# Attention scores from fp16 halves of q and k in the head loop of a decoder kernel

## What is computed

```
qkv = layernorm(x) @ w_qkv            # 16 heads of 128
scores = q @ k.T / sqrt(128)          # per sequence and head, 256 x 256
x = x + (softmax(scores) @ v) @ w_o
```

## Time and profile before

| | |
|---|---|
| median of 3 runs | 919.81 us (917.97 to 923.12) |
| time of the profiled execution | 922.4 us |
| its span, first to last instruction | 920.4 us |
| TensorE busy | 853.7 us (93%) |
| VectorE busy | 720.4 us (78%) |
| ScalarE busy | 535.1 us (58%) |
| GpSimd busy | 368.4 us (40%) |
| mean granted TensorE clock | 0.988 |
| head loop | from about 66 to 553 us of the span |

### The profile page before, as it was taken

How to read it: one execution, slowest core, us unless ns; L and a number is a source line. 1 busy time by engine, 2 the same in 40 slices (tenths; PEclk the granted TensorE clock), 3 DMA queues, 4 the chain that set the end, 5 groups by cost and what they waited for, 6 DMA issues and landing times. The chain is left out here.

```text
span 920.4 us, 18709 instructions
## 1 busy us (share of the span) xinstructions
PE 853.7 (93%) x6868; PEld 634.0 (69%) x6868; DVE 720.4 (78%) x1759; ACT 535.1 (58%) x1277; POOL 368.4 (40%) x354
## 2 busy tenths in 40 slices
PE   4788988999999999999999998999988889999786
PEld 3455766777777777777777776887855578787554
DVE  5748878878888788778887775897698779876885
ACT  1435576655665666556655744555566864545576
POOL 4103456545554455455555554043233031521410
PEclk9989999999999999999999998999999999999999
DMA  9123231011101110111000000000000010000001
GB/s 280 36 71 69 54 96 35 2 35 35 34 0 34 34 34 6 28 34 34 18 16 11 1 1 1 1 2 1 1 2 1 1 47 1 1 1 1 2 1 46
DMA packets 34722, 25.56 MB, mean 28 GB/s; under 512 B 9492, under 2 KB 31596, under 8 KB 34668
## 3 DMA queue, kind: packets, MB, share of 16 engines
q1 hardware_dynamic: 34380, 24.56, 10.3%
q10 hardware_dynamic: 288, 0.26, 0.1%
HBM read 22.65 MB, written 2.17 MB: 27 GB/s over the span
## 5 line engine op out<-in xcount | busy, mean ns | idle before, releaser
L483 POOL CAST exp_hi<-exp_scores 128x1024 f16<-128x1024 f32 x64 | 67.0, 1047 | 212.9 <-ACT exp_scores L596 212.9
L485 POOL TENSOR_TENSOR exp_lo<-exp_scores,exp_hi 128x1024 f16<-128x1024 f32 x64 | 140.7, 2199 | 5.1
L596 ACT ACTIVATE exp_scores<-banks,exp_bias,unscale 128x256 f32<-128x256 f32 x256 | 141.0, 560 | 2.1
L75 PE MATMUL banks<-value_out_hi,xn_t_hi 128*128 128x256 f16 x512 | 139.6, 273 | 0.3 <-DVE X L931 0.3
L76 PE MATMUL banks<-value_out_lo,xn_t_hi 128*128 128x256 f16 x512 | 139.6, 273 | 0.0
L77 PE MATMUL banks<-value_out_hi,xn_t_lo 128*128 128x256 f16 x512 | 139.6, 273 | 0.0
L1124 PE MATMUL banks<-qk 128*128 128x256 f32 x512 | 121.6, 380 | 9.0 <-ACT exp_scores L596 8.9
L1124 PEld LDWEIGHTS banks<-qk 128*128 128x128 f32 x512 | 96.6, 190 | 30.3 <-issue 9.6
L931 DVE SCALAR_TENSOR_TENSOR X<-banks,colsum,X 128x256 f32<-128x256 f32 x256 | 106.2, 477 | 11.0 <-DVE colsum L922 9.6
L575 ACT ACTIVATE qk<-banks 128x512 f32<-128x512 f32 x128 | 75.8, 601 | 57.9 <-PE banks L77 57.9
L906 DVE TENSOR_REDUCE neg_rowmax<-banks 128x4 f32<-128x1024 f32 x64 | 78.2, 1221 | 27.9 <-PE banks L1124 27.9
(11 more groups left out here) (253 smaller groups left out, 1973.9 us busy)
## 6 DMA issues: line engine op xcount, KB each, us to landing
head_weights<-in_wqkv_d SPq DMA_DIRECT2D x32, 128.0 KB, 3.7
weight_absmax_rows<-across_partitions SPq DMA_DIRECT2D x15, 256.0 KB, 4.0
X<-in_x_d SPq DMA_DIRECT2D x4, 512.0 KB, 7.3
head_weights<-in_wqkvt_d SPq DMA_DIRECT2D x16, 128.0 KB, 3.5
head_weights<-in_w_o_d SPq DMA_DIRECT2D x16, 128.0 KB, 3.5
out<-X SPq DMA_DIRECT2D x8, 256.0 KB, 2.1
ternary_then_kv_and_rows<-in_c_fc_d SPq DMA_DIRECT2D x1, 1024.0 KB, 6.2
ternary_then_kv_and_rows<-in_c_proj_d SPq DMA_DIRECT2D x1, 1024.0 KB, 8.0
```

Source lines behind the costliest of these rows:

```text
L75: nc.tensor.matmul(out, lhs[0], rhs[0], start=first, stop=False)
L483: nc.gpsimd.tensor_copy(probh[:, s1_.par], prob[:, s1_.par]).then_inc(exph_ready, 1)
L485: nc.gpsimd.tensor_tensor(probl[:, s1_.par], prob[:, s1_.par], probh[:, s1_.par], ALU.subtract).then_inc(expl_ready, 1)
L596: last = nc.scalar.activation(prob[:, s1_.par, t, :], sc_ps[t // ST][:, t % ST, :], ACT.Exp, bias=nbias[:, t:t + 1], scale=unscale[:, s1_. ...
```

## The change

The tile `qk` (fp32, double) is replaced by `qkh` and `qkl` (fp16, double) and a single fp32 tile `q_rows`. The scores become three fp16 products for each of the 4 tiles. ScalarE writes the upper half of q, a full copy of q into `q_rows`, and the upper half of k. GpSimd makes the lower half of q from `q_rows` and `qkh`. VectorE makes the lower half of k from PSUM and `qkh`. The semaphore `qk_ready` is split in four. TensorE's q product of the next step waits for `q_copied`, its k product for `k_lo`, and the scores wait for `q_lo` and `k_lo`.

```diff
-    qk = sb("qk", [P, 2, 2, NPAIR])
+    qkh = sb("qk_hi", [P, 2, 2, NPAIR], F16)
+    qkl = sb("qk_lo", [P, 2, 2, NPAIR], F16)
+    q_rows = sb("q_rows", [P, NPAIR])
...
-    qk_ready = sem("qk_ready")
+    qk_hi, q_copied, q_lo, k_lo = sem("qk_hi_ready"), sem("q_copied"), sem("q_lo_ready"), sem("k_lo_ready")
...
(GpSimd, after weights_lo, ahead of the halves of the exponentials)
+            if runs(i, 0):
+                pool.wait_ge(q_copied, i + 1)
+                nc.gpsimd.tensor_tensor(qkl[:, st.par, 0, :], q_rows[:, :], qkh[:, st.par, 0, :],
+                                        ALU.subtract).then_inc(q_lo, 1)
...
(ScalarE)
-                for s in range(2):
-                    act.wait_ge(qk_full, i * 2 + s + 1)
-                    nc.scalar.activation(qk[:, st.par, s, :], qk_ps[s], ACT.Copy).then_inc(qk_ready, 1)
+                act.wait_ge(qk_full, i * 2 + 1)
+                nc.scalar.activation(qkh[:, st.par, 0, :], qk_ps[0], ACT.Copy).then_inc(qk_hi, 1)
+                if not known(i) or i >= 1:
+                    act.wait_ge(q_lo, i)
+                nc.scalar.activation(q_rows[:, :], qk_ps[0], ACT.Copy).then_inc(q_copied, 1)
+                act.wait_ge(qk_full, i * 2 + 2)
+                nc.scalar.activation(qkh[:, st.par, 1, :], qk_ps[1], ACT.Copy).then_inc(qk_hi, 1)
...
(VectorE, after scales, value_out_lo and absmax, ahead of the row maximum)
+            if runs(i, 0):
+                dve.wait_ge(qk_hi, i * 2 + 2)
+                nc.vector.tensor_tensor(qkl[:, st.par, 1, :], qk_ps[1], qkh[:, st.par, 1, :],
+                                        ALU.subtract).then_inc(k_lo, 1)
...
(TensorE)
-                        pe.wait_ge(qk_ready, i * 2 - 1 + s)
+                        pe.wait_ge((q_copied, k_lo)[s], i)
...
-                pe.wait_ge(qk_ready, i * 2)
+                pe.wait_ge(q_lo, i)
+                pe.wait_ge(k_lo, i)
...
-                        last = nc.tensor.matmul(sc_ps[b][:, t, :], qk[:, s1_.par, 0, q], qk[:, s1_.par, 1, kk],
-                                                start=True, stop=True)
+                        last = pair_matmuls(nc, sc_ps[b][:, t, :], (qkh[:, s1_.par, 0, q], qkl[:, s1_.par, 0, q]),
+                                            (qkh[:, s1_.par, 1, kk], qkl[:, s1_.par, 1, kk]), True, True)
```

More of the change, by code:

```diff
@@ L1184, in gated_weights @@
                 pe.wait_ge(lv, ROUNDS * 8 * STEP_OPS)
-                pe.wait_ge(qk_ready, 2 * STEPS)
+                pe.wait_ge(q_copied, STEPS)
+                pe.wait_ge(k_lo, STEPS)
             if w >= 2:
```

## The result

The changed kernel takes 959.25 us (958.6 to 961.41, 4 runs) against 919.74: a ratio of 1.0424, 95% interval 1.0403 to 1.0445. The prediction said slower, and was right in that; its 940.3 was 19 us short, and the range to 951 did not reach the time.

A forecast was written before the change was run, and what follows sets the result against it. Bound: a chain through VectorE, ScalarE and TensorE in the long head, TensorE's own work barely above it in the short. Six bodies +17.5 and +3 outside make +20.5 us: 919.8 becomes 940.3, range 922 to 951.

The forecast's parts named there:

- d: Chain part on TensorE, start of step p = 0 to start of p = 1: 7.99 us long head, 7.98 short.
- Scores, -0.42 a head: Twelve fp16 products replace TensorE's fp32 group, 1.31 us against 1.73; the chain passes the scores once a head.
- k_lo, +0.61 twice a head: VectorE's subtraction for k ahead of the row maximum: 0.61 us, passed twice by the chain, +1.22 a head.
- a: Chain part from row maximum p = 1 to row maximum p = 2: 7.82 us long head, 7.89 short.
- e: Chain part from TensorE's start of step p = 1 to the row maximum: 4.52 us before the change.
- The rival that had `k_lo` held up: GpSimd's q subtraction delays VectorE's k subtraction at p = 1: up to +0.9 a head, 955 us; above 950: 0.06.
- q_lo, +1.0 in b: At p = 2 GpSimd's subtraction for q collides with VectorE's level part: +1.0 us a head, bounds 0 and 1.16.
- b: Chain part from row maximum p = 2 to first of 24 products of p = 3: 6.76 us long, 5.89 short.
- The rival GpSimd waits instead: GpSimd's q subtraction waits, VectorE's level part loses nothing: 928.3 us; 925 to 935, half the collisions included: 0.22.
- The granted clock: TensorE's new pauses of some 3 us a head lower its clock from 1.00; chance 0.06 shared, above 950 us.
- c: Chain part from first of the 24 products of p = 3 to TensorE's start of step p = 0: 3.03 us.
- Outside the body, +3: The 16 steps outside the six two-head bodies: +3 us in all, bounds -6.7 and +9.8.

The follow-up runs named there:

- neither: The changed kernel without both subtractions (lower halves of q and k zero, all three products and the copies kept): 910.49 us, ratio 0.9881 to the kernel before.
- fill: The changed kernel with 22 (long head) or 9 (short head) unused TensorE products ahead of the wait for X at p = 3: 950.54 us, ratio 1.0316.
- no_k_lo: The changed kernel without VectorE's subtraction for k (lower half of k zero, its product still made): 922.46 us, ratio 1.0013 to the kernel before.
- k_after_max: The changed kernel with VectorE's subtraction for k directly behind the row maximum instead of ahead of it: 964.01 us, ratio 1.0472 to the kernel before.

## Why the prediction was right in direction and short in size

- *The bound.* Right. Every part of the chain is in the profile after, and neither shows that of TensorE's 26.9 us only what lies in d comes back in the body.
- *Scores, -0.42 a head.* Right: 58.58 against 58.59 for the body.
- *k_lo, +0.61 twice a head.* Right: a is 346.29 - 337.84 = 8.45 in the long head (7.82 + 0.61 = 8.43 forecast), and e is 371.74 - 366.62 = 5.12 (5.13 forecast). The 64 subtractions take 662 to 693 ns, 685 on average, and 47 of them run beside a GpSimd instruction for more than 0.3 us, as that at 337.24 does beside the `q_lo` at 337.11. The rival that had `k_lo` held up has nothing for it. (Of the 16 cases of L704 that the prediction leaned on, only two run beside GpSimd.) The Trainium skill ("SBUF — State Buffer", § Who interferes with whom) says that a VectorE instruction with at most one SBUF input doesn't contend, outside the modes in which VectorE uses both of its port pairs; for `k_lo` the trace agrees. The prediction left that condition out, and it matters: L820 reads one SBUF tile too, and is stretched from 0.33 to 1.20. Which mode it ran in no run shows.
- *The copy to q_rows.* Hidden in the body, as said: the kernel neither makes all three copies, and its body is explained without this one.
- *q_lo, +1.0 in b.* Right in mechanism, and in the short head in size: 322.00 - 315.30 = 6.70 against 6.89. In the long head b is 354.50 - 346.29 = 8.21, against 7.76. The step that failed there is that the collision ends with `q_lo`: the level part, longer by 1, ran into the cast behind it, whose start I had not followed. The third stretched instruction costs 0.62, that by `q_lo` 0.84 instead of 1.0: 0.45 more than forecast, once a body.
- *The rival GpSimd waits instead* fell: VectorE's instructions are stretched by 0.6 to 1.0 each. At the lower weights and `q_lo` GpSimd's grow by 0.1 at most; where it does wait more (L491 took 2.65 instead of 2.13 behind the long head's L846) nothing on the path hangs on it.
- *The granted clock.* This is the main failure. I had it as a rival and gave it, with `k_lo` held up, 0.06; the sum had no term for it. The same sum already put 2.8 and 3.6 us of pauses on TensorE in a head (31.11 and 31.92 less 28.3). From 366.62 - 354.50 = 12.12, against 3.03 + 7.99 - 0.42 = 10.60, the half clock costs 1.52, once a body, all of it in c (4.55 against 3.03); fill gives 1.42 for it. That is about 9 us of the 19 missing.
- *Outside the body, +3.* Too small: 36.5 - 29.1 = 7.4 of the span, if the first body's extra 1.8 is counted here. It is inside the bounds, but I took a value too low. 5.2 of it come before the eleventh row maximum, and all of that with `k_lo`: it comes at 152.29 in no_k_lo and at 151.53 in k_after_max. From the first to the eleventh row maximum it is 87.9 us against 82.2, and three of these ten steps (the seventh, eighth and tenth) bring 1.9, 1.0 and 1.6 of it. There `k_lo` waits for a copy that stands behind a rounding of some 2 us on ScalarE; VectorE and ScalarE in the seventh:

```profile
126.32 2.00 ACT L621 ACTIVATE ternary_then_kv_and_rows<-ternary_then_kv_and_rows,ternary_rec 128x2048 f32<-128x2048 f32 x1
...
129.17 0.61 ACT L585 ACTIVATE qk_hi<-banks 128x512 f16<-128x512 f32 x1
...
129.82 0.69 DVE L916 TENSOR_TENSOR qk_lo<-banks,qk_hi 128x512 f16<-128x512 f32 x1 [3.11 <-ACT qk_hi L585]
130.43 1.22 DVE L920 TENSOR_REDUCE neg_rowmax<-banks 128x4 f32<-128x1024 f32 x1
```

VectorE idles 3.11 us for that copy, with the row maximum queued behind. The prediction named the row maximum as what is queued there, and did not ask what stands ahead of the copy outside the body.

One reckoning in the rivals was off without bearing on the outcome: with `k_lo` at nothing and the products in, the chains are 29.70 and 28.89, so 0.6 to 1.4 us more, and not 1.0 to 1.8, would have had to go for TensorE to be the bound.

In sum, by body: 2.9 forecast, + 1.5 clock, + 0.45 third collision = 4.85. Six bodies are 11.7 us more than forecast, everything else 4.4, together 16.1, and the span lies 36.5 - 20.5 = 16.0 above the forecast. The median lies 3 us further above its forecast, since the profiled execution of before was 2.6 above its median, and that of after 0.2 below.

## What to carry to other kernels

An instruction put ahead of the one on which a chain hangs costs its whole duration each time the chain passes, while a gain on the engine that looks full comes back only where the chain runs through it; measure the chain once round before pricing either. Where two engines shut each other out, count the instructions issued while the other has a string of work, not their lengths, and follow the string to its end. And when a sum opens pauses on TensorE, give the half clock behind the longest of them a price and a chance.

## What the runs showed of the hardware

- *Turns.* Beside GpSimd's back-to-back work each level instruction gets through only where one of GpSimd's ends, and then the next waits in turn: L820 of 0.33 us took 1.20, L842 of 0.52 took 1.36, L821 of 0.33 took 2.28, L846 of 0.89 took 2.60, one GpSimd instruction each. In these rows VectorE never gets two of them through in one gap. In the rows shown GpSimd's own instructions grow by 0.1 to 0.3; in others by more (L491 2.65 instead of 2.13 in after, the cast 1.70 instead of 1.04 in no_k_lo). So the price of a collision went by the number of VectorE's instructions in the string.
- *Clock.* Waits of 0.90 and 2.80 us close together, in a loop otherwise busy, were followed by half clock that cost 1.42 to 1.52 us; waits of 1.07 and 1.21, or 0.31 and 1.44, were not. The length of a wait alone doesn't decide: 2.52 in k_after_max was followed by half clock in some bodies and not in others, and 2.84 in the first body of fill (at 167.49) was not. Useless products in the second wait of the later bodies kept the clock at 1.00 and made the kernel some 8 to 10 us faster.
